# Gated delta rule of a decoder layer: key norms moved onto per-token scalars, PSUM banks dealt anew, gate masks on ScalarE, and part of the next body's start made inside the present body

## What is computed

```python
mixed = causal_conv_silu(x @ W_qkv)            # 4 taps per channel
q, k, v = split(mixed)                          # 8, 8 and 16 heads of 128
z = x @ W_z
beta = sigmoid(x @ W_b); g = -exp(A_log) * softplus(x @ W_a + dt_bias)
q = q * rsqrt(sum(q*q) + 1e-6) * DK**-0.5;  k = k * rsqrt(sum(k*k) + 1e-6)
for t in range(T):                              # per sequence and value head
    S = S * exp(g[t])
    S = S + outer(k[t], (v[t] - k[t] @ S) * beta[t])
    o[t] = q[t] @ S
o = o * rsqrt(mean(o*o) + EPS) * norm_weight * silu(z)
out = o @ W_out
```

## Time and profile before

| | us |
|---|---|
| median of 3 runs | 2410.67 |
| lowest and highest | 2406.59, 2412.37 |
| profiled execution, its time | 2405.05 |
| profiled execution, its span | 2403.3 |
| of it the 32 projecting bodies | 1450.0 |

### The profile page before, as it was taken

The page is one execution under the profiler, slowest core; times in us unless marked ns, Lnnn a source line. Parts: engine busy times, 40 slices in busy tenths (PEclk is TensorE's granted clock), DMA queues, the critical chain, the costliest instruction groups (busy, mean ns, idle before and its releaser), DMA issues. The chain is left out here.

```text
span 2403.3 us, 56028 instructions
## 1 busy us (share of the span) xinstructions
PE 2092.2 (87%) x19224; PEld 1530.1 (64%) x19224; DVE 1859.5 (77%) x4187; ACT 1433.9 (60%) x3914; POOL 1004.2 (42%) x938
## 2 busy tenths in 40 slices
PE   5799999999999999998999999858988999756998
PEld 2576776776777777776777776645656666524444
DVE  8777877887777887777877877636888888764997
ACT  2466666666666666666666666536776777633333
POOL 7434334334234334234334234213566666650332
PEclk8799999999999999999999999769999999987999
DMA  2100000000000000000000000053333333113111
GB/s 73 49 9 22 30 9 22 31 9 22 31 9 22 31 9 22 31 9 22 31 9 22 31 9 22 19 164 90 97 97 90 94 85 96 52 44 121 56 55 51
DMA packets 122857, 107.56 MB, mean 45 GB/s; under 512 B 12080, under 2 KB 97072, under 8 KB 122800
## 3 DMA queue, kind: packets, MB, share of 16 engines
q1 hardware_dynamic: 122800, 106.87, 14.3%
HBM read 72.24 MB, written 34.60 MB: 44 GB/s over the span
## 5 line engine op out<-in xcount | busy, mean ns | idle before, releaser
L601 PE MATMUL proj<-xn_hi,w_lo 128*128 x768 | 362.6, 472 | 0.0
L958 DVE SCALAR_TENSOR_TENSOR qkv<-conv_in,taps,qkv 128x512 f32<-128x512 f32 x384 | 338.0, 893 | 8.9 <-ACT qkv L830 8.9
L602 PE MATMUL proj<-xn_lo,w_hi 128*128 x768 | 307.4, 400 | 0.2 <-issue 0.2
L603 PE MATMUL proj<-xn_hi,w_hi 128*128 x768 | 306.1, 399 | 0.0
L1202 POOL TENSOR_TENSOR r_norm<-sumsq,neg_half 128x8 f32<-128x8 f32 x32 | 67.3, 2102 | 517.3 <-DVE sumsq L1118 517.3
L1173 POOL TENSOR_TENSOR o_pow<-o_var,neg_half 128x4 f32<-128x4 f32 x68 | 89.4, 1332 | 412.6 <-DVE o_var L990 412.6
L1068 DVE TENSOR_TENSOR i_less_r<-bank_c,join_mask 128x256 f16<-128x256 f32 x330 | 124.4, 417 | 113.3 <-PE bank_c L666 112.9
L884 ACT ACTIVATE inv<-bank_b 128x256 f16<-128x256 f32 x330 | 111.5, 382 | 161.7 <-PE bank_b L686 161.4
L603 PEld LDWEIGHTS proj<-xn_hi,w_hi 128*128 128x128 f32 x768 | 146.1, 190 | 35.4
L601 PEld LDWEIGHTS proj<-xn_hi,w_lo 128*128 128x128 f32 x768 | 146.0, 190 | 25.9
L1188 POOL TENSOR_TENSOR g_mask<-mask_ge,gates 128x512 fp32r<-128x512 f32 x132 | 161.0, 1251 | 0.3 <-POOLq L506 0.3
(11 more groups left out here) (288 smaller groups left out, 6103.1 us busy)
## 6 DMA issues: line engine op xcount, KB each, us to landing
out_t<-o_out SPq DMA_DIRECT2D x68, 256.0 KB, 2.0
o_raw<-out_t SPq DMA_DIRECT2D x32, 512.0 KB, 5.4
w_raw<-in_L_attn_W_qkv_dram SPq DMA_DIRECT2D x36, 256.0 KB, 2.8
wq_dram<-wq_q SPq DMA_DIRECT2D x48, 128.0 KB, 1.8
w_raw<-in_L_attn_W_z_dram SPq DMA_DIRECT2D x18, 256.0 KB, 2.7
x_sb<-in_x_dram SPq DMA_DIRECT2D x16, 256.0 KB, 2.7
x_in<-in_x_dram SPq DMA_DIRECT2D x16, 256.0 KB, 5.8
wq_raw<-in_L_ffn_w_gate_dram SPq DMA_DIRECT2D x16, 256.0 KB, 2.6
```

The source lines that it names most:

```text
L601: pe.matmul(out, w_lo[:, k, cols], sh.xn_hi[:, k, tok], start=(k == 0), stop=False)
L602: pe.matmul(out, w_hi[:, k, cols], sh.xn_lo[:, k, tok], start=False, stop=False)
L603: product = pe.matmul(out, w_hi[:, k, cols], sh.xn_hi[:, k, tok], start=False, stop=(k == KT - 1))
L958: dve.scalar_tensor_tensor(out=out, in0=conv_in[:, j, :, k:k + T], scalar=taps[:, j, k:k + 1], in1=out, op0=ALU.mult, op1=ALU.add).then_in ...
```

## The change

- k is no longer normalised. The scores are taken of the raw k; 1/|k|^2 goes into the gate columns (`key_gate`), |k| goes into the copies of v as a scale of each token (`value_copies`, six activations in place of four), q's norm goes into the epsilon of the output norm. `k_unit`, the split, the diagonals and `spread_norms` go away, with POOL's work for them.
- The gate masks are made by ACT: 16 activations of 128x128 with a column of scales each, in place of four POOL instructions of 128x512.
- `proj` is for the projection alone; decay sums, values, turned outputs and query scores use `bank_b`, the turned first factor and both results of a level use `bank_a` (one 512-wide copy in place of two of 256), first-chunk outputs use `bank_c`, so that the second `solve` now waits for the copy of `o` (`o0_done`).
- `decay_sums` of the next body stand in level 5, its key scores stand before the first outputs, and DVE makes its A and first factors in the second half of this body. The order of parts, taps, `silu`, `z_gate`, `attention` and of ACT's copies is new.

PE and ACT, cut (the first lines are of `solve` and `spread_norms`, then `step`):

```diff
-                        pe.wait_ge(x_done[s], LEVELS * (n + 1))
+                        pe.wait_ge(v_done[s], n + 1)
+                        pe.wait_ge(x_done[s], 2 * n + 2)
                     else:
+                        pe.wait_ge(o0_done[s], n + 1 + FIRST)
                         pe.wait_ge(vr_done[s], n + 1)
...
-                def spread_norms(n):
-                    for i in range(2):
-                        pe.wait_ge(diag_done, 2 * n + i + 1)
-                        last = pe.matmul(proj[0][:, :], sh.ones_r[:, :], diag[:, i, :, :], start=(i == 0), stop=(i == 1))
-                    last.then_inc(rk_ps, 1)
...
-                    scores(n)
-                    parts(0, 5)
-                    first_inverse(n)
-                    parts(5, 6)
+                    query_scores(n)
+                    parts(0, 2)
+                    first_inverse(n, 0)
+                    parts(2, 3)
+                    first_inverse(n, 1)
+                    parts(3, 4)
+                    level_r(n, 0)
+                    parts(4, 5)
+                    level_x(n, 0)
+                    parts(5, 7)
+                    level_r(n, 1)
                     values(n)
-                    parts(6, 8)
-                    for l in range(LEVELS):
-                        at, after_r, after_x = ((8, 0, 0), (8, 1, 1), (10, 1, 1), (12, 1, 1), (14, 1, 1), (16, 2, 1))[l]
-                        level_r(n, l)
-                        if l == 0:
-                            to_channels(n, projects)
-                        parts(at, at + after_r)
-                        level_x(n, l)
-                        parts(at + after_r, at + after_r + after_x)
+                    level_x(n, 1)
+                    parts(7, 8)
+                    level_r(n, 2)
+                    parts(8, 9)
+                    level_x(n, 2)
+                    parts(9, 11)
+                    level_r(n, 3)
+                    to_channels(n, True)
+                    level_x(n, 3)
+                    parts(11, 12)
+                    level_r(n, 4)
+                    parts(12, 14)
+                    level_x(n, 4)
+                    parts(14, 16)
+                    level_r(n, 5)
+                    if projects:
+                        decay_sums(n + 1, n + 1)
+                    level_x(n, 5)
+                    parts(16, 17)
+                    if projects:
+                        sums_of_squares(n)
                     for s in S:
                         solve(n, 0, s)
-                    parts(19, 20)
-                    for s in S:
-                        residual(n, 0, s)
-                    parts(20, 21)
+                    parts(17, 18)
+                    for s in S:
+                        residual(n, 0, s, projects)
+                    parts(18, 19)
                     for s in S:
                         correct(n, 0, s)
                     if projects:
-                        sums_of_squares(n)
+                        key_scores(n + 1, 3 * n + 3)
                     for s in S:
                         outputs(n, 0, s)
                         between(n, s)
+                    parts(19, 20)
+                    for s in S:
+                        solve(n, 1, s)
+                    parts(20, 21)
+                    for s in S:
+                        residual(n, 1, s, projects)
                     parts(21, 23)
                     for s in S:
-                        solve(n, 1, s)
-                    if projects:
-                        spread_norms(n)
-                    for s in S:
-                        residual(n, 1, s)
+                        correct(n, 1, s)
                     parts(23, 24)
                     for s in S:
-                        correct(n, 1, s)
-                    if projects:
-                        decay_sums(n + 1)
-                    for s in S:
...
+                def mask_gates(n, s, copied):
+
+                    if copied is not None:
+                        act.wait_ge(cols_done, copied)
+                        act.wait_ge(d_ps[s], copied)
+                    for i in range(2):
                         for hb in range(4):
-                            last = act.activation(squared[s][:, hb, :], o[s][:, hb, :], ACT.Square,
-                                                  accum_out=o_ss[s][:, hb:hb + 1])
-                        last.then_inc(oss_done[s], 1)
+                            last = act.activation(g_mask[s][:, i, hb, :], sh.mask_ge[:, :], ACT.Copy,
+                                                  scale=g_cols[:, s, 4 * i + hb:4 * i + hb + 1])
+                    last.then_inc(mask_done[s], 1)
...
+                def value_copies(n):
+                    act.wait_ge(len_done, n + FIRST)
+                    for s in S:
+                        act.wait_ge(v_ps[s], n + 1)
+                        act.activation(v_r[s][:, :, :], bank_b[s][:, 0:2, :], ACT.Copy, scale=k_len[:, 2 * s:2 * s + 1])
+                        act.activation(v[s][:, 0:2, :], bank_b[s][:, 0:2, :], ACT.Copy, scale=k_len[:, 2 * s:2 * s + 1])
+                        act.activation(v[s][:, 2:4, :], bank_b[s][:, 2:4, :], ACT.Copy,
+                                       scale=k_len[:, 2 * s + 1:2 * s + 2]).then_inc(v_done[s], 1)
...
-                    squares(n)
                     act.wait_ge(conv, CONVS * n + FIRST)
-                    act.wait_ge(rk_ps, n + FIRST)
+                    act.wait_ge(ss_ps, n + FIRST)
                     act.activation(th[:, :, :], qkv[:, 2:4, :], ACT.Tanh).then_inc(th_done, 1)
...
                     for s in S:
                         act.wait_ge(qk_done[s], n + 1)
                         act.activation(qk_off[s][:, :], bank_b[s][:, 1, :], ACT.Copy).then_inc(qk_off_done[s], 1)
+                    for s in S:
+                        inverse_turned(n, s)
+                        squares(n, s)
                     if project:
                         tile_copy(n, 0)
...
+                        if l == 1:
+                            value_copies(n)
...
-                            if l in (2, 4):
+                            if l in (1, 3):
                                 tile_copy(n, 1 + l // 2)
+                            if l == 2:
+                                for s in S:
+                                    mask_gates(n + 1, s, n + 1)
                             if l == 3:
...
                     w_copy(0)
                     if project:
-                        act.wait_ge(silu_done, 3 * n + 3)
-                        act.activation(th[:, :, :], qkv[:, 0:2, :], ACT.Square).then_inc(sq_done, 1)
-                        tile_copy(n, 4)
+                        tile_copy(n, 3)
                         if next_g is not None:
                             split(next_g, 3)
+                        tile_copy(n, 4)
+                    for s in S:
+                        act.wait_ge(o_ps[s], 2 * n + 1)
+                        act.activation(o[s][:, 0:2, :], bank_c[s][:, 0:2, :], ACT.Copy).then_inc(o0_done[s], 1)
                     for s in S:
                         act.wait_ge(v2_done[s], n + 1)
                         act.activation(v_r[s][:, :, :], v[s][:, 2:4, :], ACT.Copy).then_inc(vr_done[s], 1)
                     for s in S:
                         for e in range(2):
                             last = act.activation(o_off[s][:, e, :], bank_b[s][:, 2 + e, :], ACT.Copy,
-                                                  scale=gate[:, s, 4 + e:5 + e])
+                                                  scale=gate_off[:, s, e:e + 1])
                         last.then_inc(off_done[s], 1)
                     w_copy(1)
                     if project:
+                        key_off(n + 1, n + 1)
                         tile_copy(n, 5)
```

DVE, cut (`key_gate`, then the second half of `step`), and POOL's `step`:

```diff
+                def key_gate(n):
+
+                    dve.wait_ge(ss_ps, n + FIRST)
+                    dve.tensor_scalar(sumsq[:, :], bank_a[0][:, 3, 0:8], EPS, None, ALU.add).then_inc(ss_done, 1)
+                    dve.wait_ge(ss_done, n)
+                    dve.reciprocal(k_inv[:, :], sumsq[:, 4:8]).then_inc(inv_done, 1)
...
                     if project:
-                        dve.wait_ge(ss_ps, n + 1)
-                        dve.tensor_scalar(sumsq[:, :], proj[0][:, 0:8], EPS, None, ALU.add).then_inc(ss_done, 1)
-                    v_tap(2, 2)
+                        for s in S:
+                            key_diagonal(n + 1, s)
+                        key_gate(n + 1)
...
+                                                            scalar=gate_off[:, s, e:e + 1], in1=v[s][:, 2 + e, :],
                                                             op0=ALU.mult, op1=ALU.add)
                         last.then_inc(v2_done[s], 1)
-                    v_tap(3, 0)
+                    if project:
+                        matrix(n + 1, 0, n + 1)
+                    taps_of((3, 0))
                     if next_g is not None:
```

(21 more changed lines are left out.)

477 lines of the change are left out of this document (244 added, 233 removed).

## The result

The changed kernel takes 2671.51 us, the median of 4 runs (2666.97 to 2679.48), beside 2409.18 for the kernel before in the same comparison: a ratio of 1.110 (95% 1.108 to 1.111). The forecast was 2480, from 2370 to 2535. The direction was right; the loss, 262 us, is nearly four times the 70 forecast.

The account below looks back on a forecast made before the run. PE was taken as the bound: 40.1 us of work plus 6.35 of waits, 0.44 for boundary bodies and 0.67 for clock made 47.5 a body, 1520 over 32 against 1450 (+70), so 2480 us, range 2370 to 2535.

Parts of the forecast that it names:

- boundary bodies: Bodies where the key head changes: extra work and waits, 1.75 us per head after the change, 0.44 a body.
- waits: All PE waits walked through one body after the change, summing to 6.35 us.
- The clock: Half-clock falls behind level 4's wait, 1.3 us each, taken in half of the bodies: 0.67 us a body.
- Rival B: The clock falls more often, 1.5 falls a body: 48.9 us a body, 2524 us; chance 0.12.
- step 1: Level 0, second sequence: PE waits 1.65 us for ACT's turned inverse, ready at T + 7.05.
- four small ones: Four small DVE operations in its queue at level 0, priced at 0.5 us together.
- steps 2 and 3: Levels 3 and 4: PE waits 0.65 us behind ACT's value and tile copies, then 1.85 behind the masks.
- steps 4 and 5: Second solve waits 1.9 us for ACT's copies of z, o and v_r; second residual waits 0.3 for w's copy.
- Work of PE: PE's work without waits in an inner body: 40.1 us, with 0.8 and 0.15 removed, all else only moved.
- Rival A: Waits come out shorter and the kernel is faster: 44.1 us a body, 2371 us; chance 0.25.
- second leg: Rival A's argument that DVE's taps, freed of POOL, save 56 us of DVE, giving 2355 if DVE bounded the levels.
- signs that the prediction named: Inner body 46 to 48 us, PE busy about 40, waits on ACT, taps near 0.75, half clock behind level waits.

Follow-up runs that it names:

- best: Changed kernel with inverse copies first at level 0, masks at body start and level 0, tile 4's copy behind w's second copies: 2444.3 us.
- fill: Changed kernel, nothing moved, with 26 useless 256-column products a body placed in PE's longest waits: 2568.0 us.
- split_masks: Changed kernel with sequence 0's masks moved to where ACT idles at level 0, sequence 1's left behind level 2's copies: 2537.4 us.
- inv_first: Changed kernel with ACT's two level 0 inverse copies put ahead of the qk_off copies and the squares: 2606.3 us.
- before_masks: Kernel before with only the masks made by ACT behind level 2, gates copied by DVE: 2606.1 us; with 24 useless products filling its level 4 wait, 2508.5.
- masks_pool: Changed kernel with the masks of bodies 1 on back on GpSimd, in four operations behind its scaling of the output: 2541.5 us.
- solve_first: Changed kernel with ACT's copy of tile 4 put behind the copies of o and v_r that the second solve needs: 2657.9 us.

## Why the prediction was wrong in size

The loss is made of three terms; for each, what a body was said to take and what it took.

| term, us a body | forecast | measured | over 32 bodies |
|---|---|---|---|
| work of PE at full clock, with boundary bodies | 40.1 + 0.44 | 41.5 | +31 |
| waits | 6.35 | 7.5 | +37 |
| clock | 0.67 | 4.4 | +119 |
| body | 47.5 | 53.4 | +189 |

The 41.5 comes from best: 46.3 a body, less 3.8 of idle time and 1.0 for its stretches (half of 61 / 32). The same comes out of fill: 50.0, less 4.3, 26 x 0.12 for the products and 1.1 for its stretches. The 7.5 is (1710.00 - 1469.00) / 32, and 4.4 is what is left. It agrees with 352 / 32 = 11.0 us of half clock a body, which would cost 5.5 if PE worked all through them.

**The step that failed is "The clock"**: "I take such a fall in half of the bodies: 0.67 a body. The bounds are none, and one and a half a body (2.0)". The price of a fall was right: 1.3 forecast, and 4.4 x 32 = 141 us over 352 us of such stretches is 1.4 for 3.4 us of them. Their number was not: 83 stretches in 32 bodies, 21 of them of 6.8 us, the length of two. Only level 4's wait had been coupled to the clock, and by one example. The trace before had more to say. That example's wait was of `level_x` for DVE's `i_less_r`, not for ACT ahead of level 4, and it stands in eight bodies (1.58 to 1.61 us), of which six have the stretch and two, among them the one from 1119.10 in the earlier trace rows, do not: 0.75, not the 0.5 taken. The wait of 2.66 at `first_inverse` behind a boundary body had it in two bodies of seven, the one of 1.3 in none. The forecast itself put a wait of 1.65 at level 0 and one of 1.9 at the second solve, and gave neither a fall. Rival B named the mechanism and stopped at 1.5 falls; its true size was beyond the range. That the falls at levels 0 and 4 answer to the waits is shown by split_masks, inv_first, fill, and before_masks with and without its filling. Which waits are followed by one is not: masks_pool has waits of 2.5 us without, and the second solve's 1.63 us were followed by one in 7 bodies of 32. The late falls, 14 to 24 in most versions of the new order, are not explained by a wait; at 1.4 us each they are 20 to 34 us of the 262.

**Level 0** (step 1, 1.65): measured 2.6. There were two waits, one for each sequence, where the walk had one; DVE's tail was 1.1 us longer, since `q_eps`, one of its "four small ones" of 0.5 together, alone takes 1.13 beside GpSimd's operation. inv_first shows that ACT's order was the larger part.

**Levels 3 and 4** (steps 2 and 3, 0.65 + 1.85): measured 3.0. The masks took 4.82 for 16, 0.30 each, where I had taken 0.25. The Trainium skill (ScalarE: Activation LUTs, "What ACT_TABLE_LOAD costs"), by which they were an estimated 0.29, was nearer than the row of another operation that I chose. That masks ahead of level 4 were the wait is shown by split_masks and masks_pool.

**Second solve and residual** (steps 4 and 5, 1.9 + 0.3): measured 1.6 and none. The mechanism was right: solve_first took the v_r wait from 52.2 to 11.2 us and made the one at the residual. It was not worth its clock.

**Work of PE** (40.1): too low by 1.4, since the inner body of best has 41.48. The 0.44 taken for boundary bodies, which stands in the same row of the table, hides a part of that. Only what is removed was counted; "all else is only moved" priced the new order at nothing. That the pieces are longer because PE's sequence is cut at new places would fit, but no run tests it.

**Rival A** (faster, the waits shorter) falls with the waits, and its second leg, DVE free of POOL, shows as forecast in the taps and is worth nothing that shows, since DVE is hardly waited for (4.9 us of the 32 bodies). Most signs that the prediction named came: ACT released PE at level 0, at level 4 and at the second solve, and half clock stood behind the waits. The body was longer (51.1 us in the inner body shown, 53.4 in the mean), and PE was busy in that inner body for 44.1 instead of about 40.

## What to carry to other kernels

Price a wait on a nearly full TensorE twice: by its length, and by the stretch of half clock that can follow it; here a wait of 3.5 us in every body cost 100 us by itself and 98 by the clock. Before work is moved to an engine with idle time, look for where in its order the idle time lies: 16 small copies cost 134 us more at one place of ACT's queue than half there and half where it idled. When a trace shows one instance of an effect, count in the same trace how often its condition is met and how often the effect follows, apply that to every place that meets it, and let the range hold the case in which it follows each time.

## What was not expected of the hardware

- A stretch at half clock came with waits as short as 1.23 and 1.12 us when two stood within 3 us (level 0; at times it began inside one of them), and followed one of 2.25 in 30 bodies of 32. In masks_pool eight waits of 2.46 to 2.68 us were followed by none, and in best 15 stretches came with no idle time of more than 0.2 us in the 11 us ahead. Useless products of 256 columns (0.12 us each) in the waits of the changed kernel kept the clock at 0.98.
- A TENSOR_SCALAR of 4 columns on DVE took 1.13 us beside GpSimd's operation of 512 columns, where its neighbours of the same size took 0.16 to 0.17:

```profile
1098.66 0.16 DVE L1069 TENSOR_TENSOR gate_off<-gates,k_inv 128x4 f32<-128x4 f32 x1
1098.74 0.17 DVE L1074 COPY q_eps_last<-q_eps 128x4 f32<-128x4 f32 x1
1098.94 1.13 DVE L1076 TENSOR_SCALAR q_eps<-sumsq 128x4 f32<-128x4 f32 x1
```

  GpSimd's `ia_t` ran from 1098.8 to 1100.0 there. The Trainium skill (SBUF — State Buffer, "Who interferes with whom") has one exclusive lock for the two; the trace fits it, but no run took `ia_t` away from that place to show it.
